# An eight-expert adaLN block on one core: bounds of the FFN weights from ScalarE's sums of absolute values in place of VectorE's maxima

## What is computed

```python
h = layernorm(x) * (1 + ca) + sa
x = x + ga * attention(h)            # linear attention with a memory, width 32
h = layernorm(x) * (1 + cb) + sb
gate = softmax(h @ w_gate.T); top_k(gate, 2)
y = gelu(h @ W1[e] + b1[e]) @ W2[e] + b2[e]
x = x + gb * sum over the two experts of gate * y
```

## Time and profile before

| | us |
|---|---|
| median of three runs | 500.81 (500.67 to 501.7) |
| the profiled execution, whole time | 501.27 |
| its span in the profile | 499.4 |
| first GpSimd scatter (routing 0 done) | 105.13 |
| first FFN matmul (L1279) | 245.32 |

### The profile page before, as it was taken

One profiled execution on the slowest core, in us unless ns is written; L12 is line 12 of the kernel. 1 busy time (PEld: TensorE's weight loads), 2 busy tenths in 40 slices (PEclk: granted clock), 3 DMA queues, 4 the chain that ended last, 5 costly groups with the idle time before them and its releaser, 6 DMA issues.

```text
span 499.4 us, 13733 instructions
## 1 busy us (share of the span) xinstructions
PE 343.2 (69%) x3736; PEld 304.1 (61%) x3737; DVE 423.0 (85%) x1099; ACT 298.3 (60%) x663; POOL 306.3 (61%) x360
## 2 busy tenths in 40 slices
PE   1672565747657684763589999999999999980000
PEld 1462455637456573662379889999999999870000
DVE  2879999889998889785689888989998989888887
ACT  1362474839965985663177667677676767688100
POOL 2208820047756774766777707878888888877720
PEclk9976775869975978696599999999999999995555
DMA  8884000003322223162256645565666655534542
GB/s 213 218 332 165 1 1 0 11 27 139 105 89 80 102 99 112 59 186 73 89 156 155 144 105 133 141 143 142 142 142 143 142 142 142 133 102 123 143 114 84
DMA packets 98774, 59.61 MB, mean 119 GB/s; under 512 B 45873, under 2 KB 92081, under 8 KB 98481
## 3 DMA queue, kind: packets, MB, share of 16 engines
q1 hardware_dynamic: 90544, 42.38, 30.3%
q0 software_dynamic: 8192, 16.79, 12.5%
HBM read 21.75 MB, written 23.10 MB: 90 GB/s over the span
## 4 chain that ended last, share of the span: by engine, by line
PE 47%; DVE 32%; issue 10%; ACT 6%; DVEq 3%; ACTq 1%; POOL 0%; POOLq 0%
PE psA L1291 20%; PE psA L1279 10%; PE psV L1279 4%; PE psH L1279 4%; DVE ATT L811 3%; DVE stats L750 2%; PE psH L1177 2%; DVE X L887 2%; DVE w_parts L1020 2%; DVE stats L894 1%; PE psA L1186 1%; DVEq L1092 1%; PE psA L1188 1%; PE psA L1187 1%; DVE ROW L1099 1%
## 5 line engine op out<-in xcount | busy, mean ns | idle before, releaser
L536 POOL DMA_INDIRECT expert_rows<-ROW,POS x128 | 130.1, 1016 | 73.3 <-issue 36.6
L1291 PE MATMUL psA<-WST,ATT 128*128 x1704 | 114.0, 220 | 1.8 <-DVE ATT L1076 1.7
L1291 PEld LDWEIGHTS psA<-WST,ATT 128*128 128x128 f16 x1704 | 103.2, 98 | 8.9 <-issue 2.9
L1076 DVE SCALAR_TENSOR_TENSOR ATT<-ATT,f_scales 128x1024 f16<-128x1024 f32 x71 | 91.2, 1284 | 2.5
L551 POOL DMA_INDIRECT ROW<-expert_out,POS x64 | 69.4, 1084 | 29.8 <-issue 27.4
L694 ACT ACTIVATE ATT<-psA,b1T,f_scales 128x256 f32<-128x256 f32 x144 | 69.6, 563 | 27.6 <-PE psA L1279 27.1
L551 POOL DMA_INDIRECT BIG<-expert_out,POS x64 | 69.7, 1089 | 17.7 <-issue 16.5
L1074 DVE TENSOR_SCALAR ATT<-ATT,f_scales 128x1024 f16<-128x1024 f32 x71 | 53.8, 758 | 6.9 <-ACT ATT L694 1.8
L1279 PE MATMUL psA<-WT,WST 128*128 128x256 f16 x432 | 54.4, 277 | 2.5 <-issue 1.6
L694 ACT ACTIVATE ATT<-psV,b1T,f_scales 128x256 f32<-128x256 f32 x70 | 35.7, 561 | 30.7 <-PE psH L1279 30.7
L1177 PE MATMUL psH<-ident,ATT 128*128 128x128 f32 x64 | 14.6, 369 | 49.2 <-DVE ATT L811 49.2
(11 more groups left out here) (244 smaller groups left out, 738.7 us busy)
## 6 DMA issues: line engine op xcount, KB each, us to landing
expert_out<-VP SPq DMA_DIRECT2D x71, 128.0 KB
X<-in_x SPq DMA_DIRECT2D x8, 512.0 KB, 6.8
WST<-in_W SPq DMA_DIRECT2D x2, 2048.0 KB, 14.9
WST<-WT SPq DMA_DIRECT2D x16, 256.0 KB
out<-X SPq DMA_DIRECT2D x15, 256.0 KB
expert_rows<-ROW,POS POOLq DMA_INDIRECT x128
GA<-gate_rows SPq DMA_DIRECT2D x1, 2048.0 KB, 11.8
GA<-gate_rows SPq DMA_DIRECT2D x1, 1792.0 KB, 10.7
```

Source lines behind the costliest of these rows:

```text
L536: nc.gpsimd.indirect_dma_start(xg, bass.IndirectOffsetOnAxis(ap=POS[:, k * TILES + t:k * TILES + t + 1], axis=0), ROW[:, t * 2 * D:(t + 1) ...
L1076: nc.vector.scalar_tensor_tensor(out=GL[:, k % 2, :], in0=G[:, k % 2, :], scalar=f_scales[:, 3:4], in1=GH[:, k % 2, :], op0=ALU.mult, op1= ...
L1291: last = mm(psD[k % 2][:, h * D:(h + 1) * D], a[:, k % 2, i:i + TOK], W2S[:, ds(e * 2 * FF + b * FF + m * D, D)], start=(m == 0 and c == 0 ...
```

## The change

The bound of W1 no longer is the maximum of absolute values over its columns. ScalarE writes the absolute values of W1 (4096 columns a partition) into FOLD, a part of the ROW buffer that is not yet in use, in four ACTIVATEs of 1024 columns; GpSimd adds the upper half of FOLD to the lower three times, down to 512 columns; VectorE takes the maximum of these. So the bound is that of a sum of eight absolute values. For W2, ScalarE takes absolute values of 512 columns, one expert at a time, with the sum of them as accumulated output (`w2_sums`), and VectorE takes the maximum of the eight sums. The bounds are larger than before, and with them the scales are smaller.

The placing: `size_w1(0, 2)` behind `first_norm(1)` (behind step 0), `size_w1(2, 4)` behind step 1, `size_w2(0, 4)` behind `first_norm(2)` (behind step 2), `size_w2(4, 8)` behind step 3; the additions on GpSimd behind its constants; the two reductions on VectorE beside step 4. The wait for `w_in` moves from VectorE's step 3 to ScalarE's step 0.

```diff
@@ gpsimd @@
+            pool.wait_ge(w1_sized, 4)
+            wide = E * FF // 2
+            while wide > E * FF // 16:
+                pool_fold(nc.gpsimd.tensor_tensor(FOLD[:, 0:wide], FOLD[:, 0:wide], FOLD[:, wide:2 * wide], ALU.add))
+                wide //= 2
+
             pool.wait_ge(wb_ready, 1)
@@ scalar @@
-            steps(act, step, route, {0: lambda: first_norm(1), 2: lambda: first_norm(2), 4: lambda: act.wait_ge(ln1_ready, 3)},
+            def size_w1(a, b):
+
+                act.wait_ge(w_in, 64)
+                for k in range(a, b):
+                    part = slice(k * 2 * FF, (k + 1) * 2 * FF)
+                    nc.scalar.activation(FOLD[:, part], WST[:, 0, part], ACT.Abs).then_inc(w1_sized, 1)
+
+            def size_w2(a, b):
+
+                for e in range(a, b):
+                    ge(act, w2_sized, e)
+                    nc.scalar.activation(SIZES, WST[:, 1, e * FF:(e + 1) * FF], ACT.Abs, accum_out=w2_sums[:, e:e + 1]).then_inc(w2_sized, 1)
+
+            def first_sizes():
+                first_norm(1)
+                size_w1(0, 2)
+
+            def second_sizes():
+                first_norm(2)
+                size_w2(0, E // 2)
+
+            steps(act, step, route, {0: first_sizes, 1: lambda: size_w1(2, 4), 2: second_sizes, 3: lambda: size_w2(E // 2, E),
+                                     4: lambda: act.wait_ge(ln1_ready, 3)},
                   weights=True, last=last_rows)
@@ vector @@
-            def weight_bound(k, n, a, b):
-
-                return nc.vector.tensor_reduce(w_parts[:, k:k + 1], WST[:, n, a:b], AX.X, ALU.max, apply_absolute_value=True)
-
-            EDGE = E * FF // 4
-
-            def first_bound():
-                dve.wait_ge(w_in, 64)
-                weight_bound(0, 0, 0, EDGE)
-
-            def middle_bounds():
-                weight_bound(1, 0, EDGE, E * FF)
-                weight_bound(2, 1, 0, E * FF - EDGE)
-
             def last_bound():
-                link(weight_bound(3, 1, E * FF - EDGE, E * FF))
-                nc.vector.tensor_reduce(w_bound[:, 0:2], w_parts[:].rearrange("p (n k) -> p n k", k=2), AX.X, ALU.max)
+                dve.wait_ge(folded, 3)
+                nc.vector.tensor_reduce(w_bound[:, 0:1], FOLD[:, 0:E * FF // 8], AX.X, ALU.max)
+                dve.wait_ge(w2_sized, 8)
+                nc.vector.tensor_reduce(w_bound[:, 1:2], w2_sums[:], AX.X, ALU.max)
                 nc.vector.tensor_reduce(w_bound[:, 2:3], b1T[:], AX.X, ALU.max, apply_absolute_value=True).then_inc(wb_ready, 1)
...
-            def last_refine():
-                refine(2)
-                middle_bounds()
-
-            steps(dve, step, route, {0: second_statistics, 1: bounds_and_tiles, 2: lambda: statistics(2, SECOND_HALF + BESIDE), 3: last_refine, 4: weight_scales},
-                  weights=True, beside={2: lambda: tiles(SECOND_HALF, SECOND_HALF + BESIDE), 3: first_bound, 4: last_bound})
+            steps(dve, step, route, {0: second_statistics, 1: bounds_and_tiles, 2: lambda: statistics(2, SECOND_HALF + BESIDE), 3: lambda: refine(2), 4: weight_scales},
+                  weights=True, beside={2: lambda: tiles(SECOND_HALF, SECOND_HALF + BESIDE), 4: last_bound})
```

More of the change, by code:

```diff
@@ L171, in build_adaln_block @@
         b2B = sb("b2B", [128, E * D], f32)
-        w_parts = sb("w_parts", [128, 4], f32)
+        FOLD = ROW[:].bitcast(f32)[:, TILES * D // 2:]
+        SIZES = ROW[:].bitcast(f32)[:, TILES * D // 4:TILES * D // 4 + FF]
+        w2_sums = sb("w2_sums", [128, E], f32)
         w_bound = sb("w_bound", [128, 4], f32)
@@ L213, in build_adaln_block @@
         mr_in = [sem(f"mr_in{j}") for j in range(2)]
+        folded, w1_sized, w2_sized = sem("folded"), sem("w1_sized"), sem("w2_sized")
         bnd_ready, bnd_all, wb_ready, wb_all = sem("bnd_ready"), sem("bnd_all"), sem("wb_ready"), sem("wb_all")
@@ L502, in _ @@
                                         ALU.mult).then_inc(fold_ready, 1)
+            pool_fold = links(pool, folded, 0)
             cells = links(pool, cell_link, 0)
```

## The result

The changed kernel takes 513.59 us (median of 6 runs, 511.91 to 516.56) against 500.74 us before (6 runs beside it, 500.29 to 501.7): ratio 1.0262, 95% interval 1.0229 to 1.0294. The forecast was 514.3 us, 2.7% slower, with a range from 511.0 to 518.5.

A forecast was written before the change was run, and what follows sets the result against it. VectorE was taken to bound the attention phase, almost without waits from 34.99 to 104 us. 14.28 + 0.5 + 2.8 - 4.10 = +13.5 us on the 500.81 median gave 514.3 us, range 511.0 to 518.5.

The forecast's parts named there:

- Term 1: Step 1: ScalarE stands for the weight loads, then does two Abs passes, so VectorE's L828 comes 14.28 us later.
- the wait is none: Rival at ScalarE's new wait behind first_norm(1): ScalarE goes on at once, 500.6 us, not slower; chance 0.06.
- Term 2: Moments in step 3: GpSimd's additions hold VectorE's two-input operations, +0.5 us, bounds -1.4 to +2.8.
- the additions run from 66.98: GpSimd's three additions start when its chain ends at 66.98 and run to 71.36, 73.70 and about 75.
- GpSimd's own chain is not tied to ScalarE: GpSimd's work ahead of the additions ends at 66.98 us as before, despite ScalarE's delay.
- GpSimd does not hinder VectorE: Rival at the moments in step 3: no hindrance by the additions, -1.4 us there, 512.4 us; chance 0.14.
- Term 3: Step 3: the first four W2 sums, behind first_norm(2), are wholly on the path, +2.8 us at 0.70 each.
- reading out costs as much as a second pass: Rival at ScalarE's W2 sums: each takes 1.2 us because of the accumulator, 518.3 us; chance 0.10.
- Term 4: Step 4: the 6.61 us reduction goes, but ScalarE's last four sums take 2.5 back: -4.10 us.
- the reductions inside the steps were free: Steps 3 and 4: TensorE sets the 5.49 and 5.48 us stretches, so removing short reductions there gains nothing.
- one for one: Behind step 5: nothing later is tied to a fixed time, so VectorE's shift there shifts the end equally.
- the later stages shorten: Sign of being wrong: stages behind the first routing's POS shorten, where they were expected at the same distances.

The follow-up runs named there:

- before: The kernel without the change, the baseline: 500.74 us, median of 6 runs beside the changed kernel.
- after: The changed kernel with the whole change, against the kernel without it: 513.59 us, ratio 1.0262.

## Why the prediction was right, and where its terms were off

- **Term 1 (+14.28) holds.** The stretch from L608 to L860 grew as worked out: L860 came at 49.43 for a forecast 49.27. L608 itself starts 0.52 us later in this execution (30.38 against 29.86), so counted from there the stretch is 13.92 us longer; L860 hangs on the landing, not on L608. The landing (28.90 + 14.46 = 43.36 for 43.21) and the two passes (43.38 to 45.29, 0.95 each) came out as priced. The wait alone, measured by itself, gives 10.1 us of total because it also frees the moments. The rival "the wait is none" falls.
- **The next two passes are free,** as said: 4.82 us of idle time are left behind them.
- **Term 2 (+0.5) had the wrong sign:** from step 1 to the end of the moments the shift falls from 14.44 to 13.91, so -0.53, of which 0.30 come ahead of the moments and 0.23 in them. The step that failed is "the additions run from 66.98", and under it "GpSimd's own chain is not tied to ScalarE". That chain ended 0.9 us earlier, at 66.00. Its multiplications began 0.29 us earlier (36.18 for 36.47), and none of them was lengthened, as two pairs were in before. GpSimd and VectorE there, in the same stretch:

```profile
51.31 1.31 POOL L497 TENSOR_TENSOR BIG<-GA,memo 32x128 f32<-32x128 f32 x2
51.58 0.73 DVE L880 TENSOR_TENSOR HL<-ATT,BIG 128x512 f16<-128x512 f32 x1
```

Such a pair takes 0.97 us elsewhere. All four traces without the stall have this row of 1.31 us, both with a stall of some 7 us have it later (58.90 and 59.59), beside the same operation of VectorE, and none of the five with the whole stall has it; in three of these a small GpSimd instruction is lengthened beside that operation in its place (0.70 us for 0.32 in the run with four sums ahead), in after none. So VectorE holds GpSimd too (read from these rows, not tried by itself), and semaphores are not the only ties between the engines: a stall of ScalarE that moves VectorE moves GpSimd's chain. The second addition thus ended at 73.1, for 73.70 in the working: it held L763 by less than 0.1 us, and only the third held L764, 1.30 us. As the multiplications begin at other times in other executions, the sign is that of this execution.

That a running GpSimd instruction holds VectorE to its end, which the trace of before couldn't tell, is now shown (4.49, 2.34 and 1.13 us in a row; gone when the additions are left out). So the rival "GpSimd does not hinder VectorE" falls as a mechanism, though its 512.4 us lies 1.2 from the result and my 514.3 0.7. The Trainium skill, in "SBUF — State Buffer" (the section "Who interferes with whom"), says that whoever issues first has the port pair that the two share for the whole instruction, and the other waits. This case agrees: 4.49 us beside an addition of 4.50. The Trainium skill also names tensor_scalar there among the operations that can take the pair, which my working passed over: L843 and, with W1's own semaphore, L768 are TENSOR_SCALARs and were held for 5.34 us (four of them together) and 2.34 us.

- **Term 3 (+2.8) holds, a little low:** from the moments to L882 the shift grows by 16.79 - 13.91 = 2.88, and the sums are 0.73 to 0.76 us apart where I took 0.70. The surplus is a separate instruction, ACTIVATION_READ_ACCUMULATOR, for which the upper bound of 0.87 had left room. The rival that reading out costs as much as a second pass falls: 0.19 us.
- **Term 4 (-4.10) holds:** 12.51 - 16.79 = -4.28. What is late next is ScalarE, with a wait of 2.42 us (2.5 forecast). That the reductions inside the steps were free is shown too: from L882 of step 4 to the second L860 there are 5.49 us now (91.48 to 96.97), with a reduction of 0.67 us where there was one of 1.21, and there were 5.48. In step 3, where nothing took its place, the stretch is 5.50 us in the run without additions (78.72 to 84.22) and was 5.49; in after it is 5.24, with TensorE's clock rising inside it.
- **The sum came near in part by luck.** In the trace the four terms make 14.44 - 0.53 + 2.88 - 4.28 = 12.51 us at step 4, for 13.48 forecast. Between there and POS the shift grows to 13.00, which no term had.
- **The tail was not quite one for one,** and that the later stages shorten was among the signs of being wrong. In the two profiled executions POS is 13.0 us late and the span only 11.6 longer (by the medians it is 12.85). Some 0.8 of it come back between the second and third routing, whose POS is at 151.13 and 199.65 before and at 164.07 and 211.77 after. VectorE waits less for TensorE there, in one row of before, then of after:

```profile
162.91 0.69 DVE L842 TENSOR_TENSOR BIG<-psA,mask 128x512 f32<-128x512 f32 x1 [0.84 <-PE psA L1234]
```

```profile
175.50 0.69 DVE L874 TENSOR_TENSOR BIG<-psA,mask 128x512 f32<-128x512 f32 x1 [0.48 <-PE psA L1250]
```

Why that wait is shorter is not traced. From the first POS to the end of the span the eleven traces take 392.0 to 394.9 us, with the same instructions there, so two executions can't show that the change shortens the tail by 1.4 us.

## What to carry to other kernels

When work moves to an engine with idle time, its waits move with it and stop everything behind them in that engine's queue: place it where the engine already idles and where its data has landed. Idle time hides only what stands behind the thing waited for; look at which side of it the new work falls. And a long two-input GpSimd instruction held VectorE's TENSOR_TENSOR and TENSOR_SCALAR on SBUF here until it ended: its price is how much of it they run into, not how early its result is needed. Not every operation is held: in after the 18 BATCH_NORM_STATS2 from 69.24 run beside the first two additions in 3.54 us, and without additions they take the same.

## What was not expected of the hardware

- A sum with an accumulated output is two instructions on ScalarE: the ACTIVATE of 512 columns (0.61 to 0.63 us) and a read of the accumulator (0.19 to 0.20), 0.73 to 0.76 us from one to the next.
- VectorE's TENSOR_SCALAR, with one tensor input, is held by GpSimd like a TENSOR_TENSOR: 0.18 us became 2.34. The SCALAR_TENSOR_TENSOR at 73.91, where the second addition ended, took its usual 0.20; whether it came first or is not held, this row doesn't tell.
- The hold goes both ways: a pair of GpSimd multiplications took 1.31 us in place of 0.97 beside VectorE's L880.
- TensorE can take back what a shorter wait gives: with four sums ahead it started 2.3 us sooner, ran that block at 1.2 GHz to its end (the granted clock is 0.50 up to 84.2) and lost 1.1 us.
